# Hyperbolic attention of a four-layer model: constant products added on TensorE, the second batch's scores and turns reordered

## The chip, the cores and the metric

The kernel is one program on one core of a Trainium2 chip. Its time is the device time of one execution in microseconds (us), and of several executions the median. The engines are called PE (matmul), DVE (vector), ACT (scalar functions), POOL (GpSimd) and SP (which issues transfers).

## The reference, cut to what matters

A model of four layers, each with cross attention, self attention and a feed-forward block, on B = 2 sequences of T = 256 tokens and 256 channels. The change touches one block of it, the self attention of layer 1, with H = 16 heads of 16 channels:

```python
importance = jax.nn.sigmoid(x @ Wimp.T + bimp)
spikes = (importance > spike_threshold).astype(x.dtype)
spike_mask = spikes.reshape(B, 1, T, 1)
...
scores_euclid = jnp.einsum('bhtd,bhsd->bhts', q, k) / math.sqrt(D)
...
q_hyp = _expmap0(qn)
k_hyp = _expmap0(kn)
inner = -jnp.einsum('bhti,bhsi->bhts', q_hyp[..., :1], k_hyp[..., :1]) + jnp.einsum('bhtd,bhsd->bhts', q_hyp[..., 1:], k_hyp[..., 1:])
mdot = jnp.maximum(-inner, 1.0 + 1e-06)
dist = jnp.arccosh(mdot)
scores_hyper = -(dist * dist) / curv_k
scores = (1.0 - alpha) * scores_euclid + alpha * scores_hyper
scores = jnp.where(causal[None, None], scores, -jnp.inf)
attn = jax.nn.softmax(scores, axis=-1) * spike_mask
y = jnp.einsum('bhts,bhsd->bhtd', attn, v)
return y @ Wout.T + bout
```

## The kernel before, in words

`hyperbolic_attention` projects q, k, v and the gates, maps q and k to points of the hyperboloid, and turns them so that channels lie on partitions (`turned["qE"]`, `["kE"]` the plain ones, `["qH"]`, `["kH"]` the points). Then `hyperbolic_softmax` makes everything from the inner products to the scaled y. It is one stage: each engine has a program written out by hand, and semaphores order them.

Work goes in 16 pairs of heads, 8 to a batch; two pairs make a quad (8 quads). Of a head's 256 x 256 scores the causal part is kept, W = 384 columns: 128 for the first block of queries, 256 for the second. A pair so has 768 columns, in two PSUM banks. `banks` has three such slots. The list `order` says which piece of work takes the next slot ("hyper" products, "plain" scores, "turn"), and `slot_free` waits until the piece three places ahead has been read.

A pair passes these steps. PE multiplies points (L1916, hyper). DVE makes reach, max(m, 1 + 1e-6) - 1, (L1982) and the radicand of arccosh (L1986). ACT takes the root (L2038), POOL adds it (L2028), ACT takes the logarithm (L2043), POOL squares it (L2031). PE puts a constant causal mask (`steps16_q`, 384 columns a head, bf16, L1923) and the plain products (L1916) into a slot. DVE adds the two kinds of score (L2010, four operations) and finds the maxima (L2015, two). ACT takes exponentials (L2062, four). PE turns the six 128 x 128 blocks (L1931), ACT copies them out (L2047). For each quad PE multiplies by v (values, L1942; column 16 of each 32 holds the softmax's sum), ACT copies y (L2053), PE spreads the sums over the rows with a selecting matrix (L1952), and DVE inverts them (L1991), multiplies by the spikes (L1993) and by y (L1995). The spikes were spread at the stage's start by four matmuls (L1955) and an ACT copy (L2072).

The order: PE multiplies the points of all 16 pairs. Then, for each batch, two scores ahead, and for each pair the scores of the pair two on, the turn, and after each second pair values or spread_sums. DVE does all reaches and radicands, then a batch's scorings with a normal() after each second one. ACT does the roots and logarithms of batch 0, the roots of batch 1, the exponentials and copies of batch 0, the logarithms of batch 1, and its exponentials and copies. Roots, logarithms and exponentials each need their own table, loaded when the function changes.

## Time and profile before

| | |
|---|---|
| three executions | 2756.8, 2743.03, 2754.75 us, median 2754.75 |
| profiled execution | 2750.46 us, its span 2748.6 us |
| mean granted clock of PE | 0.895 of full speed |
| busy shares of the span | PE 85%, DVE 53%, ACT 38%, POOL 14% |
| the stage that the change touches | 1557.70 to 1661.90, 104.20 us, 3.8% of the span |

The profile is of one execution. A granted clock of 1.00 is 2.4 GHz, of 0.50 is 1.2 GHz. "x24" behind a row is its count of instructions; a float32 matmul appears twice in it. In a timeline the bracket at the end is the idle time ahead, and what ended it. A window's row gives its stretch and length, the busy us (xcount) of PE, PEld (PE's weight loads), DVE, ACT and POOL, the granted clock, the DMA share and GB/s.

### The profile page before, as it was taken

The numbers are of one execution on the slowest core, as the hardware profiler recorded it, in microseconds if no ns is written. First come the engines' busy times: TensorE is split into PE (matmuls) and PEld (weight loads), VectorE is DVE, ScalarE is ACT, GpSimd is POOL, SyncE is SP. The second block draws the span as 40 slices with busy tenths as digits, with TensorE's granted clock in tenths as the row PEclk, the third lists the DMA queues.
The fourth block names the chain that finished last, engine by engine and source line by source line (L and its number), as shares of the span: only waits on it lengthen the run. The fifth ranks groups of instructions, "written<-read, shape, count | busy, mean of one in ns | idle before, by whom it ended". The sixth has DMA issues, their size and how long they took to land. (4 is left out here: it accounts for less than half of the span.)

```text
span 2748.6 us, 38678 instructions
## 1 busy us (share of the span) xinstructions
PE 2333.9 (85%) x15024; PEld 1363.0 (50%) x15024; DVE 1455.3 (53%) x2285; ACT 1055.1 (38%) x1896; POOL 380.9 (14%) x659
## 2 busy tenths in 40 slices
PE   3999999868999698999996684886889799697778
PEld 1344444435699463454443443352238557364447
DVE  4777777423221356888883684225877332223333
ACT  2566666512111233777774371123432133021310
POOL 2453000000000400000001250001630000000100
PEclk8899999978899897999998777886989899898889
DMA  7977543020353698556430001001004430200200
GB/s 192 237 183 160 119 90 58 12 96 1 138 229 140 221 281 244 108 93 127 93 59 34 12 1 59 28 1 63 0 19 166 168 123 1 96 1 2 99 1 8
DMA packets 108213, 258.59 MB, mean 94 GB/s; under 512 B 11808, under 2 KB 83072, under 8 KB 94080
## 3 DMA queue, kind: packets, MB, share of 16 engines
q1 hardware_dynamic: 101696, 203.71, 28.2%
q0 software_dynamic: 2736, 39.37, 4.2%
...
## 5 line engine op out<-in xcount | busy, mean ns | idle before, releaser
L666 DVE TENSOR_REDUCE sta_parts<-sta_psA 128x1 f32<-128x1024 f32 x544 | 625.6, 1187 | 188.6 <-PE sta_psA L583 186.8
L724 ACT ACTIVATE sta_probs<-sta_psS 128x512 f32<-128x512 f32 x1056 | 575.8, 597 | 274.9 <-PE sta_psS L594 272.8
L594 PE MATMUL sta_psS<-L_xattn_qS,L_xattn_kst 99*128 99x256 bf16 x2112 | 356.3, 278 | 11.5 <-ACT sta_probs L724 6.6
L583 PE MATMUL sta_psA<-L_xattn_kst,L_xattn_qS 99*128 99x512 bf16 x1088 | 293.3, 387 | 46.9 <-PEq L59 32.1
L594 PEld LDWEIGHTS sta_psS<-L_xattn_qS,L_xattn_kst 99*128 99x128 bf16 x2112 | 161.4, 98 | 259.5 <-ACT sta_probs L724 183.3
L603 PE MATMUL sta_psO<-sta_probs,L_xattna_V 128*32 128x256 f32 x2560 | 189.5, 385 | 0.0
L583 PEld LDWEIGHTS sta_psA<-L_xattn_kst,L_xattn_qS 99*128 99x128 bf16 x1088 | 104.3, 99 | 131.7 <-DVE sta_parts L666 43.7
L202 ACT ACT_TABLE_LOAD x14 | 18.0, 1283 | 327.7 <-PEq L59 327.7
L603 PE MATMUL sta_psO<-sta_probs,L_xattn_V 128*32 128x256 f32 x1536 | 114.8, 390 | 0.0
L1008 ACT ACTIVATE sht_probs<-sht_psS 128x768 f32<-128x768 f32 (+1 forms) x64 | 55.3, 863 | 148.8 <-PE sht_psS L852 99.7
L443 POOL CAST sta_split<-sta_neg 128x2 bf16<-128x2 f32 x64 | 12.1, 188 | 715.9 <-issue 467.5
L603 PEld LDWEIGHTS sta_psO<-sta_probs,L_xattna_V 128*32 128x32 f32 x2560 | 82.4, 109 | 51.4 <-issue 20.9
L2415 POOL TENSOR_TENSOR l2t_u<-l2s_rowsB,l2s_dx 128x512 f32<-128x512 f32 x64 | 80.2, 1266 | 139.7 <-POOLq L59 99.3
L953 DVE TENSOR_REDUCE sht_neg<-sht_psM 128x2 f32<-128x512 f32 (+1 forms) x128 | 69.3, 583 | 41.4 <-PE sht_psM L845 41.4
L2385 PE MATMUL l2t_psY<-l2t_hc,top_consts_weights 128*128 128x512 f32 x128 | 77.0, 699 | 15.0 <-DVE l2t_hc L2431 14.9
L823 POOL MEMSET sht_Z<- 128x512 bf16 x4 | 2.1, 526 | 593.0 <-POOLq L59 593.0
L2424 DVE TENSOR_TENSOR_SCAN l2t_h<-l2t_decay,l2t_u 128x512 f32<-128x512 f32 x64 | 76.4, 1214 | 11.7 <-ACT l2t_decay L2397 9.3
L255 PE MATMUL gem_banks<-3f_L_ffn_experts_weights,l3f_hT 128*128 128x256 f32 x288 | 64.3, 387 | 12.4 <-PEq L59 12.4
L1710 DVE TENSOR_TENSOR l0f_inner_hT<-exp_psG,l0f_inner_gel 128x512 f32<-128x512 f32 x22 | 15.2, 691 | 97.4 <-ACT l0f_inner_gel L1636 97.4
L255 PEld LDWEIGHTS gem_banks<-3f_L_ffn_experts_weights,l3f_hT 128*128 128x128 f32 x288 | 56.0, 195 | 21.1 <-issue 13.2
L603 PEld LDWEIGHTS sta_psO<-sta_probs,L_xattn_V 128*32 128x32 f32 x1536 | 49.5, 110 | 31.8 <-issue 14.0
L1170 PE MATMUL prj_psV<-L_xattn_L_xattn_weights,L_xattnq_cxT 128*128 128x256 f32 x256 | 59.9, 388 | 4.9 <-DVE prj_rows L1210 4.9
...
## 6 DMA issues: line engine op xcount, KB each, us to landing
...
L_xattna_V<-L_xattn_values SPq DMA_DIRECT2D x5, 2048.0 KB, 11.1
...
```

What stands on the lines that cost most here:

```text
L255: last = nc.tensor.matmul(view(n), *term, start=i == 0, stop=i == len(terms) - 1)
L583: last = nc.tensor.matmul(psA[:, u % 2, col:col + rhs.shape[1]], lhsT, rhs, start=True, stop=True)
L594: last = nc.tensor.matmul(psS[:, at % 2, j * T:(j + 1) * T], lhsT, rhs, start=True, stop=True)
L603: last = nc.tensor.matmul(psO[32 * group:32 * group + 32, 0:T], v, probs[:, u % NP, col:col + T], start=first, stop=final)
L666: nc.vector.tensor_reduce(into(parts[:, u // n % 2]), view(psA[:, u % 2, :]), AX.X, ALU.max).then_inc(max_taken, 1)
L724: nc.scalar.activation(probs[:, u % NP, i * 512:(i + 1) * 512], psS[:, at % 2, :], ACT.Exp, scale=scale).then_inc(probs_ready, 1)
L953: last = nc.vector.tensor_reduce(neg[:, g % 2, t, 2 * (u % 2):2 * (u % 2) + 2], psM[:, u % 2, :, at:at + w], AX.X, ALU.max, negate=True)
L1008: nc.scalar.activation(probs[:, u % NP, :, 0:W], psS[:, :, 0:W], ACT.Exp, scale=scale).then_inc(probs_ready, 1)
L1170: last = nc.tensor.matmul(psV[:, v % VRING, j * C:(j + 1) * C], cxT[b][:, k, t * P:(t + 1) * P], w["v"][:, k, 0:C], start=k == 0, stop=k = ...
L2385: nc.tensor.matmul(psY[:, m, :], K["ident"], hc[:, i % 3, :], start=s == 0, stop=s == NS - 1).then_inc(summed, 1)
L2415: nc.gpsimd.tensor_tensor(u[:, i % 3, :], rowsB[:, s % ROWS, :], dx[:, m, :], ALU.mult).then_inc(input_ready, 1)
L2424: nc.vector.tensor_tensor_scan(h[:, i % 3, :], decay[:, i % 2, :], u[:, i % 3, :], 0.0, ALU.mult, ALU.add).then_inc(states_ready, 1)
```

## The change: what it does

1. The spread spikes go. The sums are inverted as columns: two matmuls of 4 columns (`sums`, into the free part of psY), a reciprocal of 8 columns and two products with the spikes (`invert`), an ACT copy that repeats each value 32 times (`widen`), two matmuls that turn the result (`spread`), and one product on DVE (`scale`). psY and psN have one buffer each.
2. `fill` multiplies a constant by a constant, bf16, 384 columns; nothing reads the result. Two follow each pair of points, two stand ahead of each of the second batch's scores, and twelve ahead of each batch's first turn.
3. The mask is added on the diagonal blocks only, 4 x 128 columns a pair.
4. The second batch's scores and scorings stand together beside its logarithms, all its turns after them, and the copies of its turns are on DVE (`copied_by_dve`) rather than ACT.

```diff
-    order = [("hyper", k) for k in range(PAIRS)]
-    for b in range(B):
-        own = range(b * HALF, (b + 1) * HALF)
-        order += [("plain", own[0]), ("plain", own[1])]
-        for k in own:
-            order += [("plain", k + 2)] * (k + 2 in own) + [("turn", k)]
+    order = [("hyper", k) for k in range(PAIRS)] + [("plain", 0), ("plain", 1)]
+    for k in range(HALF):
+        order += [("plain", k + 2)] * (k + 2 < HALF) + [("turn", k)]
+    order += [("plain", k) for k in range(HALF, PAIRS)] + [("turn", k) for k in range(HALF, PAIRS)]
...
-        spikesT = p.sb("spikesT", [P, NTOK])
         yP = p.sb("yP", [P, 2, T])
-        inverse = p.sb("inverse", [P, 2, T])
+        inverse = p.sb("inverse", [P, 2, TB, 4])
+        wide = p.sb("wide", [P, 2, T])
         banks = p.ps("banks", [P, 2 * SLOTS, 512])
-        psY = p.ps("psY", [P, 2, T])
-        psN = p.ps("psN", [P, 2, T])
+        psY = p.ps("psY", [P, 512])
+        psN = p.ps("psN", [P, T])
...
+                def fill(dst, n):
+
+                    for _ in range(n):
+                        nc.tensor.matmul(dst, K["ident16"], K["mask16_q"][:, 0:W], start=True, stop=True)
...
+                def points(k):
+                    slot_free("hyper", k)
+                    dst = pair("hyper", k)
                     for t in range(TB):
                         for j in range(2):
-                            r = slice(64 * half + 32 * j, 64 * half + 32 * j + 32)
-                            last = nc.tensor.matmul(dst[:, j, cols[t]], q[r, c, (b * TB + t) * P:(b * TB + t + 1) * P],
-                                                    k[r, c, b * T:b * T + (t + 1) * P], start=first, stop=first or t == TB - 1)
-                    return last
+                            last = product(dst, turned["qH"], turned["kH"], k, j, t, start=True, stop=True)
+                    last.then_inc(hyper_ready, 1)
+                    fill(psY[:, 0:W], 2)
 
                 def scores(k):
                     slot_free("plain", k)
+                    dst = pair("plain", k)
+                    if k >= HALF:
+                        fill(dst[:, 0, :], 2)
                     for j in range(2):
-                        nc.tensor.matmul(pair("plain", k)[:, j, :], K["ident16"], K["steps16_q"], start=True, stop=False)
-                    products(pair("plain", k), turned["qE"], turned["kE"], k, False).then_inc(plain_ready, 1)
+                        product(dst, turned["qE"], turned["kE"], k, j, 1, start=True, stop=False)
+                    for j in range(2):
+                        nc.tensor.matmul(dst[:, j, 2 * P:W], K["ident16"], K["steps16_q"][:, 2 * P:W], start=False, stop=True)
+                    for j in range(2):
+                        nc.tensor.matmul(dst[:, j, 0:P], K["ident16"], K["steps16_q"][:, 0:P], start=True, stop=False)
+                    for j in range(2):
+                        last = product(dst, turned["qE"], turned["kE"], k, j, 0, start=False, stop=True)
+                    last.then_inc(plain_ready, 1)
 
                 def turn(k):
                     slot_free("turn", k)
+                    if k % HALF == 0:
+                        fill(pair("turn", k)[:, 0, :], 12)
                     pe.wait_ge(exp_ready, k + 1)
...
+                    copied(2 * g + 1)
                     if g:
                         pe.wait_ge(y_copied, g)
+                        pe.wait_ge(inverse_in, g)
...
+                def sums(g):
+
                     pe.wait_ge(y_copied, g + 1)
+                    for t in range(TB):
+                        last = nc.tensor.matmul(psY[:, T + 4 * t:T + 4 * t + 4], yP[:, g % 2, t * P:(t + 1) * P], K["col32"], start=True, stop=True)
+                    last.then_inc(sums_ready, 1)
+
+                def spread(g):
+                    pe.wait_ge(widened, g + 1)
                     if g:
-                        pe.wait_ge(inverted, g)
-                    else:
-                        pe.wait_ge(spikes_copied, 1)
-                    nc.tensor.matmul(psN[:, g % 2, :], K["sel32"], yP[:, g % 2, :], start=True, stop=True).then_inc(spread_ready, 1)
-
-                for t in range(NT):
-                    last = nc.tensor.matmul(psN[:].rearrange("p a n -> p (a n)")[:, t * P:(t + 1) * P], spikes[:, t:t + 1].to_broadcast([P, P]), K["ident"],
-                                            start=True, stop=True)
-                last.then_inc(spikes_spread, 1)
+                        pe.wait_ge(scaled, g)
+                    for t in range(TB):
+                        last = nc.tensor.matmul(psN[:, t * P:(t + 1) * P], wide[:, g % 2, t * P:(t + 1) * P], K["ident"], start=True, stop=True)
+                    last.then_inc(spread_ready, 1)
...
+                    points(k)
+                scores(0)
+                scores(1)
+                for k in range(HALF):
+                    if k + 2 < HALF:
+                        scores(k + 2)
+                    turn(k)
+                    if k % 2 == 0 and k:
+                        values(k // 2 - 1)
+                    if k % 2 == 0 and k > 2:
+                        spread(k // 2 - 2)
+                    if k % 2 and k > 1:
+                        sums((k - 3) // 2)
+                values(QHALF - 1)
+                spread(QHALF - 2)
+                scores(HALF)
+                sums(QHALF - 1)
+                scores(HALF + 1)
+                scores(HALF + 2)
+                spread(QHALF - 1)
+                for k in range(HALF + 3, PAIRS):
+                    scores(k)
+                for k in range(HALF, PAIRS):
+                    g = k // 2
+                    turn(k)
+                    if k % 2 == 0 and k > HALF:
+                        values(g - 1)
+                    if k % 2 == 0 and k > HALF + 2:
+                        spread(g - 2)
+                    if k % 2 and k > HALF + 1:
+                        sums(g - 1)
+                values(QUADS - 1)
+                spread(QUADS - 2)
+                sums(QUADS - 1)
+                spread(QUADS - 1)
...
+                def invert(g):
+                    b = g // (QUADS // B)
+                    dve.wait_ge(sums_ready, g + 1)
+                    V.reciprocal(inverse[:, g % 2], psY[:, T:T + 4 * TB].rearrange("p (t h) -> p t h", t=TB)).then_inc(inverse_in, 1)
+                    dve.wait_ge(inverse_in, g + 1)
+                    for t in range(TB):
+                        last = V.tensor_scalar(inverse[:, g % 2, t], inverse[:, g % 2, t], spikes[:, b * TB + t:b * TB + t + 1], None, ALU.mult)
+                    last.then_inc(inverted, 1)
+
+                def scale(g):
                     b, c = g // (QUADS // B), g % (QUADS // B)
                     dve.wait_ge(spread_ready, g + 1)
-                    V.reciprocal(inverse[:, g % 2, :], psN[:, g % 2, :]).then_inc(inverted, 1)
-                    dve.wait_ge(inverted, g + 1)
-                    V.tensor_tensor(inverse[:, g % 2, :], inverse[:, g % 2, :], spikesT[:, b * T:(b + 1) * T], ALU.mult).then_inc(inverse_ready, 1)
-                    dve.wait_ge(inverse_ready, g + 1)
-                    V.tensor_tensor(attT[:, c, b * T:(b + 1) * T], yP[:, g % 2, :], inverse[:, g % 2, :], ALU.mult).then_inc(scaled, 1)
+                    V.tensor_tensor(attT[:, c, b * T:(b + 1) * T], psN[:], yP[:, g % 2, :], ALU.mult).then_inc(scaled, 1)
...
+                def copy_turned(k):
+                    dve.wait_ge(turn_ready, k + 1)
+                    V.tensor_copy(both(R, k), pair("turn", k)).then_inc(copied_by_dve, 1)
+
+                for k in range(HALF):
+                    scored(k)
+                    if k % 2 == 0 and k >= 4:
+                        invert(k // 2 - 2)
+                    if k % 2 == 0 and k >= 6:
+                        scale(k // 2 - 3)
+                invert(QHALF - 2)
+                scale(QHALF - 3)
+                scale(QHALF - 2)
+                scored(HALF)
+                scored(HALF + 1)
+                invert(QHALF - 1)
+                for k in range(HALF + 2, PAIRS):
+                    scored(k)
+                    if k == HALF + 4:
+                        scale(QHALF - 1)
+                for k in range(HALF, PAIRS):
+                    copy_turned(k)
+                    if k % 2 == 0 and k >= HALF + 4:
+                        invert(k // 2 - 2)
+                    if k % 2 == 0 and k >= HALF + 6:
+                        scale(k // 2 - 3)
+                invert(QUADS - 2)
+                scale(QUADS - 3)
+                scale(QUADS - 2)
+                invert(QUADS - 1)
+                scale(QUADS - 1)
...
+                def widen(g):
+                    act.wait_ge(inverted, g + 1)
+                    nc.scalar.copy(wide[:, g % 2, :].rearrange("p (x n) -> p x n", n=32),
+                                   inverse[:, g % 2].rearrange("p t h -> p (t h)").unsqueeze(2).to_broadcast([P, 4 * TB, 32])).then_inc(widened, 1)
+
+                def weights(k):
+                    act.wait_ge(top_ready, k + 1)
+                    for j in range(2):
+                        for t in range(TB):
+                            one = D[:, 2 * k + j, cols[t]]
+                            last = nc.scalar.activation(one, one, ACT.Exp, bias=top[:, k, t, j:j + 1])
+                    last.then_inc(exp_ready, 1)
+
                 roots(0)
-                logarithms(0)
+                logarithms(range(HALF))
                 roots(1)
-                weights(0)
-                logarithms(1)
-                weights(1)
+                for k in range(HALF):
+                    weights(k)
+                    if k:
+                        copy_turned(k - 1)
+                        if k % 2 and k > 1:
+                            copy_y((k - 3) // 2)
+                        if k % 2 and k >= 5:
+                            widen((k - 5) // 2)
+                copy_turned(HALF - 1)
+                widen(QHALF - 2)
+                logarithms(range(HALF, HALF + 1))
+                copy_y(QHALF - 1)
+                logarithms(range(HALF + 1, HALF + 4))
+                widen(QHALF - 1)
+                logarithms(range(HALF + 4, PAIRS))
+                for k in range(HALF, PAIRS):
+                    g = k // 2
+                    weights(k)
+                    if k % 2 and k > HALF + 1:
+                        copy_y(g - 1)
+                    if k % 2 and k >= HALF + 5:
+                        widen(g - 2)
+                widen(QUADS - 2)
+                copy_y(QUADS - 1)
+                widen(QUADS - 1)
```

PE at the stage's start. Before, the spike matmuls and then the points' products:

```order
L1955 MATMUL hyp_psN<-top_consts_weights,l1a_spikes 128x128 x4
L1916 MATMUL hyp_banks<-l1a_T_kH,l1a_T_qH 128x128 x2
L1916 MATMUL hyp_banks<-l1a_T_kH,l1a_T_qH 128x256 x2
L1916 MATMUL hyp_banks<-l1a_T_kH,l1a_T_qH 128x128 x2
L1916 MATMUL hyp_banks<-l1a_T_kH,l1a_T_qH 128x256 x2
```

Now, the same products (L1928) with two constants (L1923) behind each pair's:

```order
L1928 MATMUL hyp_banks<-l1a_T_kH,l1a_T_qH 128x128 x2
L1928 MATMUL hyp_banks<-l1a_T_kH,l1a_T_qH 128x256 x2
L1923 MATMUL hyp_psY<-top_mask,top_ident 128x384 x2
L1928 MATMUL hyp_banks<-l1a_T_kH,l1a_T_qH 128x128 x2
L1928 MATMUL hyp_banks<-l1a_T_kH,l1a_T_qH 128x256 x2
L1923 MATMUL hyp_psY<-top_mask,top_ident 128x384 x2
```

The spikes' four are gone, and each pair's block is followed by 768 columns of constants.

PE in the second batch. Before, a score (L1923, L1916), a turn (L1931), and after each second pair values (L1942) or spread (L1952):

```order
L1931 MATMUL hyp_banks<-top_consts_weights,hyp_D 128x128 x6
L1942 MATMUL hyp_psY<-hyp_R,l1a_v 32x256 x4
L1942 MATMUL hyp_psY<-hyp_R,l1a_v 32x128 x4
L1923 MATMUL hyp_banks<-top_steps,top_ident 128x384 x2
L1916 MATMUL hyp_banks<-l1a_T_kE,l1a_T_qE 128x128 x2
L1916 MATMUL hyp_banks<-l1a_T_kE,l1a_T_qE 128x256 x2
L1931 MATMUL hyp_banks<-top_consts_weights,hyp_D 128x128 x6
L1952 MATMUL hyp_psN<-hyp_yP,top_consts_weights 128x256
```

Now, the end of its last score, the twelve constants, the first three turns in a row, and the first values and sums (L1982):

```order
L1928 MATMUL hyp_banks<-l1a_T_kE,l1a_T_qE 128x256 x2
L1948 MATMUL hyp_banks<-top_steps,top_ident 128x128 x2
L1950 MATMUL hyp_banks<-top_steps,top_ident 128x128 x2
L1928 MATMUL hyp_banks<-l1a_T_kE,l1a_T_qE 128x128 x2
L1923 MATMUL hyp_banks<-top_mask,top_ident 128x384 x12
L1962 MATMUL hyp_banks<-top_consts_weights,hyp_D 128x128 x18
L1974 MATMUL hyp_psY<-hyp_R,l1a_v 32x256 x4
L1974 MATMUL hyp_psY<-hyp_R,l1a_v 32x128 x4
L1962 MATMUL hyp_banks<-top_consts_weights,hyp_D 128x128 x6
L1982 MATMUL hyp_psY<-top_consts_weights,hyp_yP 128x4 x2
```

All eight scores of the batch now stand ahead of its first turn.

DVE at the end of the second batch. Before, the last scoring's two last additions (L2010), its maxima (L2015) and the normalisations:

```order
L2010 SCALAR_TENSOR_TENSOR hyp_D<-hyp_R,l1a_coef,hyp_banks 128x128
L2010 SCALAR_TENSOR_TENSOR hyp_D<-hyp_R,l1a_coef,hyp_banks 128x256
L2015 TENSOR_REDUCE hyp_top<-hyp_D 128x2 x2
L1991 RECIPROCAL hyp_inverse<-hyp_psN 128x256
L1993 TENSOR_TENSOR hyp_inverse<-hyp_inverse,hyp_spikesT 128x256
L1995 TENSOR_TENSOR l1a_attT<-hyp_yP,hyp_inverse 128x256
```

Now, all eight copies of turns (L2078) behind the last scoring, among inverses (L2045, L2048) and a scale (L2054):

```order
L2068 SCALAR_TENSOR_TENSOR hyp_D<-hyp_R,l1a_coef,hyp_banks 128x256
L2073 TENSOR_REDUCE hyp_top<-hyp_D 128x2 x2
L2078 COPY hyp_R<-hyp_banks 128x768 x5
L2045 RECIPROCAL hyp_inverse<-hyp_psY 128x8
L2048 TENSOR_SCALAR hyp_inverse<-hyp_inverse,l1a_spikes 128x4 x2
L2078 COPY hyp_R<-hyp_banks 128x768 x2
L2045 RECIPROCAL hyp_inverse<-hyp_psY 128x8
L2048 TENSOR_SCALAR hyp_inverse<-hyp_inverse,l1a_spikes 128x4 x2
L2054 TENSOR_TENSOR l1a_attT<-hyp_psN,hyp_yP 128x256
```

The first inverse of the batch stands behind five copies.

## Rows read from the trace of the kernel before

**Rows 1.** Windows of the stage: busy us (xcount) by engine, clock, DMA share, GB/s

```profile
1557.70:1594.30 36.60, 30.93 (x166) 17.17 (x167) 34.05 (x48) 25.49 (x33) 30.18 (x19) 0.57 0.07 22
1594.30:1620.74 26.44, 23.04 (x168) 14.31 (x168) 19.77 (x40) 17.42 (x40) 9.69 (x6) 0.75 0.00 1
1620.74:1661.90 41.16, 28.24 (x202) 17.00 (x202) 34.45 (x66) 28.31 (x54) 11.80 (x8) 0.79 0.00 1
```

**Rows 2.** Timeline of PE at the stage's start: start, us, engine, line

```profile
1558.01 1.13 PE L1955 MATMUL hyp_psN<-top_consts_weights,l1a_spikes 128*128 128x128 f32 x8 [1.05 <-PEq L59]
1559.07 1.58 PE L1916 MATMUL hyp_banks<-l1a_T_kH,l1a_T_qH 32*128 32x128 f32 x24
```

**Rows 3.** Timeline of DVE, the first hyper operation and the first scoring

```profile
1560.04 1.82 DVE L1982 TENSOR_SCALAR hyp_D<-hyp_banks 128x768 f32<-128x768 f32 x2 [2.35 <-PE hyp_banks L1916]
...
1588.41 1.38 DVE L2010 SCALAR_TENSOR_TENSOR hyp_D<-hyp_R,l1a_coef,hyp_banks 128x128 f32<-128x128 f32 x4
```

**Rows 4.** Timeline of PE: scores, turns, a spread and values at either clock

```profile
1585.95 0.82 PE L1923 MATMUL hyp_banks<-top_steps,top_ident 128*128 128x384 bf16 x2 [0.19 <-DVE hyp_R L1986]
...
1588.29 0.82 PE L1923 MATMUL hyp_banks<-top_steps,top_ident 128*128 128x384 bf16 x2
...
1594.32 1.51 PE L1931 MATMUL hyp_banks<-top_consts_weights,hyp_D 128*128 128x128 f32 x6 [1.30 <-ACT hyp_D L2062]
...
1605.63 0.88 PE L1931 MATMUL hyp_banks<-top_consts_weights,hyp_D 128*128 128x128 f32 x6
1606.34 0.60 PE L1952 MATMUL hyp_psN<-hyp_yP,top_consts_weights 128*128 128x256 f32 x2
...
1608.86 0.86 PE L1942 MATMUL hyp_psY<-hyp_R,l1a_v 128*32 128x256 f32 x16
...
1621.42 0.49 PE L1923 MATMUL hyp_banks<-top_steps,top_ident 128*128 128x384 bf16 x2
...
1622.70 0.50 PE L1923 MATMUL hyp_banks<-top_steps,top_ident 128*128 128x384 bf16 x2
```

**Rows 5.** Windows, columns as in rows 1, for the granted clock

```profile
1563.30:1585.90 22.60, 20.70 (x102) 11.34 (x98) 22.46 (x27) 15.99 (x19) 21.78 (x14) 0.50 0.00 1
1585.95:1592.90 6.95, 6.95 (x30) 3.17 (x30) 6.88 (x15) 6.92 (x10) 6.95 (x5) 0.50 0.00 0
1620.90:1625.30 4.40, 4.39 (x32) 2.27 (x32) 4.30 (x5) 4.39 (x5) 2.25 (x2) 1.00 0.01 4
1768.70:1771.40 2.70, 2.62 (x20) 1.29 (x20) 1.02 (x2) 1.28 (x1) 0.52 (x1) 0.98 0.62 177
1771.50:1774.00 2.50, 0.24 (x3) 0.25 (x4) 0.96 (x2) 0.00 (x0) 0.87 (x4) 0.50 1.01 381
```

**Rows 6.** Timeline of ACT at the second batch's start and the stage's end

```profile
1620.74 1.28 ACT L2043 ACT_TABLE_LOAD   x1
1622.04 6.71 ACT L2043 ACTIVATE hyp_D<-hyp_D,top_consts_weights 128x768 f32<-128x768 f32 x8
...
1630.06 2.88 ACT L2062 ACTIVATE hyp_D<-hyp_D,hyp_top 128x128 f32<-128x128 f32 x8
...
1657.84 0.37 ACT L2053 COPY hyp_yP<-hyp_psY 128x256 f32<-128x256 f32 x1 [0.98 <-PE hyp_psY L1942]
```

**Rows 7.** Timeline of DVE around the second batch's start

```profile
1620.80 0.42 DVE L1993 TENSOR_TENSOR hyp_inverse<-hyp_inverse,hyp_spikesT 128x256 f32<-128x256 f32 x1
...
1623.41 1.38 DVE L1993 TENSOR_TENSOR hyp_inverse<-hyp_inverse,hyp_spikesT 128x256 f32<-128x256 f32 x1
...
1626.32 1.38 DVE L2010 SCALAR_TENSOR_TENSOR hyp_D<-hyp_R,l1a_coef,hyp_banks 128x128 f32<-128x128 f32 x4
1627.74 1.01 DVE L2015 TENSOR_REDUCE hyp_top<-hyp_D 128x2 f32<-128x256 f32 x2
```

**Rows 8.** Groups by form, busy us and mean ns of one: small operations elsewhere

```profile
L969 DVE RECIPROCAL sht_inverse<-sht_psT 128x16 f32<-128x16 f32 x10 | 2.6, 258 | 22.9 <-PE sht_psT L914 22.9
...
L914 PE MATMUL sht_psT<-top_consts_weights,l0a_attT 128*128 128x4 f32 x32 | 4.9, 280 | 0.5 <-ACT l0a_attT L994 0.5
```

106 lines of the change are left out of this document (38 added, 68 removed).

## The prediction

> **What bounds the kernel now.** I read the windows first. The change touches one stage of a kernel with some dozens of stages, the hyperbolic softmax, which lasts from 1557.70 to 1661.90 us: 104.2 us. Cut at its first turn and at the table load of the second batch's logarithms it falls into A 36.60, B 26.44 and C 41.16 us [rows 1]. Whatever the change does has to come out of these. No engine fills all three: DVE is busy 34.05 of 36.60 us in A, 19.77 of 26.44 in B and 34.45 of 41.16 in C [rows 1]. So DVE bounds A, and B and C are hand-overs between PE, DVE and ACT.
>
> The timeline of A shows DVE going without a gap from the first hyper operation at 1560.04 to the first scoring at 1588.41 [rows 3]; that is 32 operations (two a pair) in 28.37 us, 0.89 us each, so 1.77 us a pair; from 1563.30 to 1585.90 it is busy 22.46 of 22.60 us [rows 5]. PE works at 1.2 GHz there (granted 0.50) and just keeps up. Its pieces have two prices: a score piece (two constants of 384 columns and a pair's products) takes 2.34 us at 1.2 GHz (1585.95 to 1588.29) and 1.28 at 2.4 GHz (1621.42 to 1622.70); six turns take 1.51 or 0.88 [rows 4]. So the clock decides whether the longer PE programme hides.
>
> **The change, part A.** The four spike matmuls go: the first product stood at 1559.07 behind their start at 1558.01 [rows 2], so all starts 1.06 us sooner, DVE at 1558.98. Then each pair gets two constants behind its products. These are the same constants and the same number of products as a score piece, so the price is 2.34 or 1.28 us against DVE's 1.77. At 2.4 GHz it is hidden (the cover is DVE; the first scoring then comes at 1558.98 + 28.37 = 1587.35, 1.1 us sooner); at 1.2 GHz it is not, and PE becomes the bound.
>
> Will the clock hold? Three rows speak. Pieces of this very make, back to back, kept 2.4 GHz while they lasted: 1620.90 to 1625.30, granted 1.00. The same pieces at 1.2 GHz, PE busy 6.95 of 6.95 us, did not raise it: granted 0.50 from 1585.95 to 1592.90. And in a later stage two such pieces in 2.70 us ran at 0.98 and the granted clock was 0.50 right behind them [rows 5]. Paced by DVE the new pieces come at most two in 3.54 us, thinner than that last case. So I expect the clock to fall while the points run, as it did before, only some pairs later, and then not to come back as long as nothing but such pieces runs. The Trainium skill (TensorE: Matmul & The Clock Gate, Part 1) says that the default state is throttled and activity releases it, and advises to keep TensorE busy; read simply, filling PE with constants would hold 2.4 GHz. The row of 6.95 busy us at 0.50 is the case in this trace that does not follow from being busy alone. What holding it would give is the first rival.
>
> I take six pairs before the fall: three ahead at 1.28 (to 1561.8), three at DVE's pace (to 1567.1), then ten at 2.34, to 1590.5. A new score piece has the same products and two thirds of the constants' columns: 2.34 less a third of the 0.82 of its two constants [rows 4], 2.1 us (bounds 1.28 and 2.34). The first scoring starts at 1592.5 instead of 1588.41, and three pieces end at 1596.8. Ahead of the first turn come twelve more constants: from 0.49 / 2 = 0.25 each at 2.4 GHz to 0.82 / 2 = 0.41 each at 1.2 [rows 4], so 2.9 to 4.9 us; I take 4.1, since the rows' durations hold an end that overlaps with the next. The first turn starts at 1600.9 instead of 1594.3. ACT's exponentials are ready sooner than that (first scoring 1592.5 + 2.4 + 1.4), so PE is what is late. **A: +6.5.**
>
> **Part B.** The constants lie dense ahead of the turns, and I give them the clock back: turns, values and spreads at 2.4 GHz where the first three turns were at 1.2. The normalisation changes from reciprocal and two products over 256 columns (DVE) to a tiny sum on PE (two matmuls of about 0.28), a reciprocal of 8 columns (bounded by 0.26 for 16), two small products, a widening copy on ACT (256 columns, like copy_y's 0.37) and two spread matmuls [rows 4, 6, 8]. DVE's part shrinks, but the chain now goes through PE and ACT twice, psY is one buffer (values(g) waits for the reciprocal of g-1), and spread(g) and invert(g) stand in queues ahead of scores and scorings. A clock gain of at most 3 turns x 0.63 + 3 pieces x 1.06 = 5.1 stands against those hand-overs; I take them as equal (bounds -4 and +3).
>
> The two small products read and write SBUF alone, and POOL, with the second batch's sums, is still busy for 9.69 us of B [rows 1]. A 256-column product between SBUF operands took 0.42 us at 1620.80 and 1.38 at 1623.41, when POOL had begun its squares (2.25 us of POOL end the window that closes at 1625.30) [rows 5, 7]. I take +1.0 for it. The Trainium skill (SBUF — State Buffer, Who interferes with whom) has this as a rule: a DVE instruction with two SBUF inputs or in a two-port mode waits for GpSimd's whole instruction. The trace agrees (0.42 against 1.38). **B: +1.0** (bounds -4 and +4).
>
> **Part C.** The second batch's scorings move beside its logarithms, the turns' copies to DVE, all after the last scoring. Step by step at 2.4 GHz, from the table load:
> First scoring: load 1.28, first logarithm 0.84 (6.71 / 8), a square, which lies between 0 and 3.4 (5.58 us from load to first scoring before [rows 6, 7], less 2.1) and which I take as 1.5, hand-overs 0.2: 3.8.
> Eight scorings of 1.38 + 1.01 less 0.05 of overlap [rows 7]: 18.8, and 1.5 for an inverse, a scale and a wait for logarithms behind widen: 20.3.
> Tail. ACT has exponentials 8 to 11 behind it, then copy_y(4), and everything behind that waits: copy_y(4) needs values(4), values(4) needs two copies that DVE starts only now. Two copies 1.9 (one bounded by DVE's 0.91 on as many PSUM columns [rows 3]), values 0.86, copy_y 0.37, four exponentials 1.44, turn 0.88, copy 0.95, hand-overs 0.5: first inverse after 6.9. Each further quad goes round values 0.86, copy_y 0.37, widen 0.4, spread 0.5, turn 0.88, two copies 1.9 less overlap 0.1, inverse 0.3 [rows 3, 4, 6, 8]: 5.1, twice. Last: values, copy_y, sum, inverse, widen, spread, scale, 4.0. Tail 21.1.
> Sum 45.2 against 41.16: +4.0 even at 2.4 GHz, since DVE's work is not less and the tail is a chain.
> Now the clock. While scoring, PE has two constants (0.75) and a 2.1 us piece per pair at 1.2 GHz, 2.9 against DVE's 2.35: eight are 23.2, +3.4 with the waits beside. By the argument of A these are thin pieces of the same make at DVE's pace, so I take 1.2 GHz. In the tail each loop has 0.63 for a turn more at 1.2 GHz, as much for values and some 0.4 for a spread (an estimate, by the same ratio), 1.7 a loop; twelve constants stand ahead of it, so I take one loop of the three, +1.6. **C: +9.0.**
>
> **Sum.** 6.5 + 1.0 + 9.0 = +16.5. The profiled execution took 2750.46 us (span 2748.6), 4.3 below the median of the runs shown (2743.03 to 2756.8, mean 2751.5): 2767.0. DMA and other stages aren't touched. What moves behind the stage is only where the clock's changes fall, a few us of either sign.
>
> **The rivals.**
> Clock held: 2.4 GHz throughout, as the rule above and the row 1620.90 to 1625.30 suggest. A -1.1, B 0, C +4.0: 2753. Against it the row behind 1771.4. It decides as soon as nine of the ten late pairs run at 1.28.
> Constants never bring the clock back, also not ahead of the turns: A +7.3 (twelve at 0.41), B +6 (eight turns x 0.63 and two spreads), C +11 (a second loop): 2775. For it speaks that 6.95 busy us did not raise it; against it that those had the thin products, and twelve constants have not.
> Overlap pays (the other side): the tail isn't a chain but DVE's own work, 8 x 0.9 + 4 x 0.9 = 11, in place of 21, and the clock holds: C -6, A -1.1, and B at its lower bound -4: -11.1, 2739. It needs ACT to get past copy_y(4) within 1 us of the last scoring; the order rows say that it can't.
> No effect: clock held in A alone, lost in C: A -1.1, B +1, C +9: 2759.
>
> **How the numbers follow.** Chances: forecast 0.50 (its own range +10 to +23), held 0.22, never back 0.12, mixed 0.10, overlap pays 0.06. 0.5% is 13.8 us, about what a measurement of this kernel tells from no change. Of the forecast two thirds lie above it, and all of "never back": slower 0.33 + 0.12 + 0.01 = 0.46. Held, mixed and the forecast's lower third: same 0.47. Faster 0.07. The range leaves out the far ends of the outer rivals: 2746 to 2781.
>
> **What would show it.** In the profile after: DVE's first scoring near 1592, not 1587; granted clock falling to 0.50 between 1566 and 1570 and PE without gaps until about 1600; first turn near 1601; in C an ACT gap of some 8 us ahead of a copy_y while DVE copies; stage length about 120 us. Wrong if the granted clock stays 1.00 through the points, if the second batch's tail is under 15 us, or if a stage outside moves.

## The result, and the profile after

The changed kernel takes 2767.36 us (median of 8, 2762.27 to 2778.03), the kernel before 2750.44 (median of 8). The ratio is 1.0073, with a 95% interval of 1.0054 to 1.0091: slower by some 20 us by the ratio, 17 by the medians. A second set of the same program gave 1.0096 (1.0073 to 1.0119). The forecast was 2767.0.

The profiled execution took 2762.76 us (span 2760.8, clock 0.898). Its stage runs from 1554.12 to 1683.23: 129.1 us, against 104.2. Cut where [rows 1] are cut, and with the pairs at the lower clock as a fourth row (columns as there), the windows of the changed kernel are:

```profile
1554.12:1595.77 41.65, 39.95 (x209) 18.81 (x210) 35.33 (x50) 26.60 (x35) 35.47 (x22) 0.63 0.07 20
1595.77:1624.41 28.64, 21.74 (x185) 16.02 (x187) 14.36 (x42) 16.38 (x39) 4.36 (x3) 0.85 0.00 1
1624.41:1683.23 58.82, 50.68 (x292) 31.52 (x284) 31.42 (x77) 24.05 (x52) 11.48 (x8) 0.62 0.00 1
1564.90:1592.30 27.40, 27.34 (x128) 12.59 (x126) 22.77 (x32) 21.05 (x26) 26.57 (x17) 0.50 0.00 1
```

A is 41.65 us against 36.60, B 28.64 against 26.44, C 58.82 against 41.16. DVE's (VectorE's) busy time fell in B (14.36 against 19.77) and C (31.42 against 34.45), yet both grew: DVE waits more. In all, +24.9 us against a forecast of +16.5, of which C makes 17.7. That the total came out as forecast is partly luck. The stage starts 3.6 us sooner in this execution, and what lies behind it is 9 us shorter, though the edit doesn't touch either. The windows from the stage's end to the same table load in a later layer, and from there to the end, of the changed kernel and then of the kernel before:

```profile
1683.23:2058.18 374.95, 287.60 (x1056) 124.26 (x1056) 200.43 (x300) 101.92 (x150) 87.69 (x97) 0.87 0.08 28
2058.18:2760.80 702.62, 583.17 (x3096) 412.46 (x3096) 259.50 (x661) 151.65 (x256) 15.52 (x67) 0.88 0.18 67
```

```profile
1661.90:2046.95 385.05, 300.55 (x1056) 129.83 (x1056) 200.31 (x300) 101.91 (x149) 87.75 (x97) 0.82 0.07 27
2046.95:2748.60 701.65, 582.94 (x3096) 411.80 (x3096) 259.36 (x661) 151.64 (x256) 15.52 (x67) 0.89 0.18 67
```

TensorE's counts are the same, and in the first window the granted clock is 0.87 instead of 0.82, for 10.1 us less. So the forecast had the stage 8.4 us too short, and what lies outside it made up for that. It does not do so reliably: over the fourteen traces of this document the span less the stage lies anywhere from 2632 to 2651 us, though no edit touches what is in it. The kernel before lies between 2737.9 and 2756.8 us by itself. Below I therefore compare stages, and give the ratio beside.

Part A, TensorE's timeline of the changed kernel, where the clock falls:

```profile
1562.88 0.50 PE L1923 MATMUL hyp_psY<-top_mask,top_ident 128*128 128x384 bf16 x2
1563.75 0.92 PE L1928 MATMUL hyp_banks<-l1a_T_kH,l1a_T_qH 32*128 32x128 f32 x8 [0.37 <-DVE hyp_R L2040]
1564.61 0.81 PE L1923 MATMUL hyp_psY<-top_mask,top_ident 128*128 128x384 bf16 x2
1565.48 1.65 PE L1928 MATMUL hyp_banks<-l1a_T_kH,l1a_T_qH 32*128 32x128 f32 x8
1567.07 0.82 PE L1923 MATMUL hyp_psY<-top_mask,top_ident 128*128 128x384 bf16 x2
1567.82 1.65 PE L1928 MATMUL hyp_banks<-l1a_T_kH,l1a_T_qH 32*128 32x128 f32 x8
```

Two constants take 0.50 us up to the sixth pair, 0.81 behind the seventh (1564.61) and 0.82 from there on; from there TensorE has no gap, and each pair takes 2.34 us (1565.48 to 1567.82). Twelve constants at 1592.32 take 3.61 us and the clock is back: the turns behind them take 0.82 to 0.88 us.

Part B, DVE's inverses in the changed kernel, with what they waited for:

```profile
1604.31 0.21 DVE L2045 RECIPROCAL hyp_inverse<-hyp_psY 128x8 f32<-128x8 f32 x1 [1.52 <-PE hyp_psY L1982]
1604.56 0.36 DVE L2048 TENSOR_SCALAR hyp_inverse<-hyp_inverse,l1a_spikes 128x4 f32<-128x4 f32 x2
...
1614.06 0.21 DVE L2045 RECIPROCAL hyp_inverse<-hyp_psY 128x8 f32<-128x8 f32 x1 [4.46 <-PE hyp_psY L1982]
...
1623.35 0.21 DVE L2045 RECIPROCAL hyp_inverse<-hyp_psY 128x8 f32<-128x8 f32 x1 [6.02 <-PE hyp_psY L1982]
```

They come 9.8 and 9.3 us apart, and DVE is idle 4.46 and 6.02 us ahead of them. On ACT and on TensorE in the same place:

```profile
1607.29 1.49 ACT L2151 ACTIVATE hyp_D<-hyp_D,hyp_top 128x128 f32<-128x128 f32 x4 [2.29 <-DVE hyp_top L2073]
...
1609.37 0.36 ACT L2139 COPY hyp_yP<-hyp_psY 128x256 f32<-128x256 f32 x1
1609.63 0.41 ACT L2143 COPY hyp_wide<-hyp_inverse 128x256 f32<-128x256 f32 x1
```

```profile
1607.07 0.86 PE L1974 MATMUL hyp_psY<-hyp_R,l1a_v 128*32 128x256 f32 x16
1610.09 0.71 PE L1990 MATMUL hyp_psN<-top_consts_weights,hyp_wide 128*128 128x128 f32 x4 [2.16 <-ACT hyp_wide L2143]
...
1612.11 1.27 PE L1962 MATMUL hyp_banks<-top_consts_weights,hyp_D 128*128 128x128 f32 x6
1613.17 0.86 PE L1982 MATMUL hyp_psY<-top_consts_weights,hyp_yP 128*128 128x4 f32 x4
...
1620.16 1.22 PE L1990 MATMUL hyp_psN<-top_consts_weights,hyp_wide 128*128 128x128 f32 x4 [3.74 <-ACT hyp_wide L2143]
```

The wait goes round: the inverse waits for sums (L1982), which stand behind spread (L1990), the next score and a turn; spread waits for widen (L2143); widen stands behind the exponentials of pair 5 and a copy of y; and those exponentials wait for a scoring that stands behind the inverse before.

Part C, DVE in the changed kernel, from the last two scorings on:

```profile
1650.79 1.39 DVE L2068 SCALAR_TENSOR_TENSOR hyp_D<-hyp_R,l1a_coef,hyp_banks 128x128 f32<-128x128 f32 x4 [0.74 <-PE hyp_banks L1928]
...
1653.96 1.39 DVE L2068 SCALAR_TENSOR_TENSOR hyp_D<-hyp_R,l1a_coef,hyp_banks 128x128 f32<-128x128 f32 x4 [0.74 <-PE hyp_banks L1928]
...
1658.11 2.69 DVE L2078 COPY hyp_R<-hyp_banks 128x768 f32<-128x768 f32 x3 [1.71 <-PE hyp_banks L1962]
...
1664.57 0.20 DVE L2045 RECIPROCAL hyp_inverse<-hyp_psY 128x8 f32<-128x8 f32 x1
...
1671.54 0.20 DVE L2045 RECIPROCAL hyp_inverse<-hyp_psY 128x8 f32<-128x8 f32 x1
...
1676.65 0.20 DVE L2045 RECIPROCAL hyp_inverse<-hyp_psY 128x8 f32<-128x8 f32 x1
...
1682.69 0.43 DVE L2054 TENSOR_TENSOR l1a_attT<-hyp_psN,hyp_yP 128x256 f32<-128x256 f32 x1 [1.75 <-PE hyp_psN L1990]
```

Each scoring waits 0.74 us for TensorE and they come 3.17 us apart. Behind the last one 26.7 us go by, where the kernel before had 8.9.

### The profile page after: what moved, and what is told of

The parts are those of the page before. It is cut to its first block and busy times, and to the rows that moved or that the text cites. A ratio compares the mean times of both kernels' runs of the same rounds, so it can differ in the third digit from the quotient of the medians.

```text
span 2760.8 us, 38981 instructions
## 1 busy us (share of the span) xinstructions
PE 2347.6 (85%) x15168; PEld 1373.2 (50%) x15168; DVE 1448.8 (52%) x2301; ACT 1051.0 (38%) x1895; POOL 380.5 (14%) x659
## 5 line engine op out<-in xcount | busy, mean ns | idle before, releaser
L603 PEld LDWEIGHTS sta_psO<-sta_probs,L_xattna_V 128*32 128x32 f32 x2560 | 82.8, 109 | 52.0 <-issue 21.9
L2488 PE MATMUL l2t_psY<-l2t_hc,top_consts_weights 128*128 128x512 f32 x128 | 73.6, 664 | 16.7 <-DVE l2t_hc L2534 16.5
L255 PE MATMUL gem_banks<-3f_L_ffn_experts_weights,l3f_hT 128*128 128x256 f32 x288 | 64.3, 387 | 12.5 <-PEq L59 12.5
```

The source lines that it names most:

```text
L255: last = nc.tensor.matmul(view(n), *term, start=i == 0, stop=i == len(terms) - 1)
L603: last = nc.tensor.matmul(psO[32 * group:32 * group + 32, 0:T], v, probs[:, u % NP, col:col + T], start=first, stop=final)
L2488: nc.tensor.matmul(psY[:, m, :], K["ident"], hc[:, i % 3, :], start=s == 0, stop=s == NS - 1).then_inc(summed, 1)
```

## The experiments

"Stage" is from TensorE's first instruction of the stage to DVE's last; A ends at the first turn, B at the table load of the second batch's logarithms. Each stage is one traced execution, each ratio is to the kernel before over 6 to 12 executions of the variant, with its interval.

| kernel | A | B | C | stage | ratio |
|---|---|---|---|---|---|
| before | 36.3 | 26.4 | 41.0 | 103.8 | 1 |
| changed | 41.3 | 28.6 | 58.7 | 128.7 | 1.0073 (1.0054 to 1.0091) |
| a_again | 40.2 | 29.1 | 59.6 | 128.8 | 1.0096 (1.0073 to 1.0119) |
| a_nopoints | 36.2 | 28.7 | 58.7 | 123.5 | 1.0061 (1.0038 to 1.0084) |
| a_noscores | 41.1 | 31.0 | 53.4 | 125.5 | 1.0054 (1.0035 to 1.0072) |
| a_nofill | 35.2 | 33.8 | 54.4 | 123.4 | 1.0041 (1.0024 to 1.0058) |
| a_three | 35.4 | 33.5 | 58.7 | 127.5 | 1.0094 (1.0077 to 1.0111) |
| a_exps | 42.3 | 27.8 | 54.3 | 124.4 | 1.0070 (1.0052 to 1.0088) |
| b_points | 36.4 | 26.4 | 41.0 | 103.8 | 1.0001 (0.9987 to 1.0015) |
| b_diag | 36.3 | 27.6 | 42.4 | 106.4 | 1.0013 (0.9999 to 1.0027) |
| n_order | 35.2 | 37.5 | 50.1 | 122.8 | 1.0074 (1.0055 to 1.0094) |
| n_late | 35.2 | 26.8 | 38.9 | 101.0 | 1.0001 (0.9987 to 1.0014) |
| n_late_fill | 42.3 | 22.2 | 45.1 | 109.6 | 1.0017 (0.9997 to 1.0036) |
| b_warm | 36.4 | 21.4 | 41.4 | 99.2 | 0.9993 (0.9974 to 1.0011) |

**The constants, taken out one by one.** a_nopoints:

```diff
-                    fill(psY[:, 0:W], 2)
```

> The changed kernel without the two constants behind each pair's points; all else as changed. Theory (at 1.2 GHz the constants make PE the bound of part A): DVE's 32 operations run without a gap again, the first scoring starts 0.96 + 28.4 us after PE's first product, 5.2 us sooner than in the changed kernel, and the stage is 5 us shorter than its 129.1 us. Rival (the constants cost nothing there, PE would be late anyway because of the clock, or the normal order of scores): the first scoring stays at 34.6 us after the first product. Second rival (the constants feed the clock, so that what follows gets dearer without them): the first scoring is sooner, but part B loses more than 5 us.

A is 5.2 us shorter (the first scoring 29.4 us after the first product, not 34.6), B and C are unchanged: the theory, to the tenth of a microsecond in the stage. The ratios, 1.0073 and 1.0061, can't tell it from nothing.

a_noscores:

```diff
-                    if k >= HALF:
-                        fill(dst[:, 0, :], 2)
```

> The changed kernel without the two constants ahead of each score of the second batch. Theory (each scoring waits for PE, 3.17 us a piece at 1.2 GHz, of which the constants are 0.75): the pieces come each 2.43 us, DVE's own 2.35 nearly bounds them, the eight scorings take 26.9 - 8 x 0.75 = 20.9 us and the stage is 6 us shorter. Rival (the constants keep the clock from being worse, or the scorings wait for the squares): no gain, the scorings keep their distance of 3.17.

The eight scorings take 22.6 us instead of 26.9, C 5.3 less. B is 2.4 us longer, though it ends before the edit's first instruction; its granted clock is 0.77, against 0.85. The stage gains 3.2, half of what was expected.

a_nofill takes out these two and the twelve:

```diff
-                    if k % HALF == 0:
-                        fill(pair("turn", k)[:, 0, :], 12)
```

> The changed kernel with none of its constants: no fill behind points, ahead of scores, or ahead of the turns. Theory (the thin constants only cost, the twelve pay for themselves through the clock): -5 in part A, -6 in the second batch's scorings, the first turns 3 us sooner each but at 1.2 GHz (1.5 us instead of 0.9, values 1.5 instead of 0.86), which gives back some 8 us in parts B and C: stage about 115 to 118 us. Rival (the clock doesn't need the twelve): stage 129.1 - 5 - 6 - 3 - 3.4 = 112 us or less with turns at 0.88. Second rival (order and hand-overs, not the constants, are the cost): stage above 120 us.

123.4 us: neither the 115 to 118 of the theory nor 112, but the second rival. A and C fall by 6.1 and 4.3, and B rises by 5.1, with a granted clock of 0.65 instead of 0.85: without the twelve the first turns start at 1.2 GHz. All constants together cost 5.3 us of the 24.9; the other 19.6 are elsewhere.

**Does the clock fall among the points by the program?** b_points puts the constants into the kernel before:

```diff
                     products(pair("hyper", k), turned["qH"], turned["kH"], k, True).then_inc(hyper_ready, 1)
+                    for _ in range(2):
+                        nc.tensor.matmul(psY[:].rearrange("p a n -> p (a n)")[:, 0:W], K["ident16"], K["mask16_q"][:, 0:W], start=True, stop=True)
```

> The kernel before with only two constants of 384 columns (bf16) behind each pair's points. Theory: PE needs 2.34 us a pair at 1.2 GHz against DVE's 1.77, with the clock falling after about seven pairs, so the first scoring comes 5 us later after PE's first product than in the kernel before (30.4 us) and the stage takes 109 us instead of 104.2. Rival (the clock holds at 2.4 GHz, where the pair costs 1.28): the stage keeps 104 us or is 2 us shorter, since the first turns run at 2.4 GHz.

The rival. The window of its points, and that of a_three below:

```profile
1560.48:1587.09 26.61, 21.55 (x161) 10.18 (x161) 25.31 (x30) 16.83 (x20) 21.44 (x14) 1.00 0.10 30
```

```profile
1561.08:1588.50 27.42, 24.73 (x181) 12.07 (x182) 25.96 (x30) 16.90 (x20) 22.10 (x14) 1.00 0.10 29
```

Granted 1.00 throughout. In b_points these are the same pieces as in the changed kernel, three close together and then one each 1.73 us; there the clock fell behind the seventh. But nothing is won: DVE bounds A, TensorE then waits 4.35 us for the exponentials, and the first turns run at 1.2 GHz all the same.

a_three:

```diff
-                    fill(psY[:, 0:W], 2)
+                    fill(psY[:, 0:W], 3)
```

> The changed kernel with three constants instead of two behind each pair's points. Two executions with two constants ended differently: the clock fell after the seventh pair in the changed kernel, and held to the last pair in the kernel before with the same pieces. Theory (more constants keep the clock safely at 2.4 GHz, and then PE's 1.5 us a pair hides behind DVE's 1.73): granted 1.00 to the last pair, first scoring 29.4 us after the first product instead of 34.6, stage 5 us shorter. Rival (it falls all the same): PE needs 2.72 us a pair at 1.2 GHz, the first scoring comes at 38 us or later and the stage is 3 to 4 us longer.

The theory on A: 35.4 us. But B is 33.5 instead of 28.6 (granted 0.66 there, not 0.85), so that only 1.2 us of the stage is left of it, and the ratio is no better. The twelve constants are in this run too, so they don't secure the clock of B by themselves. B's instructions are the same in six of these runs, and its length goes with its granted clock: 27.8 us at 0.93 (a_exps), 28.6 and 28.7 at 0.85 (changed, a_nopoints), 29.1 at 0.78 (a_again), 31.0 at 0.77 (a_noscores), 33.5 at 0.66 (a_three).

a_again is the changed kernel, unaltered.

> The changed kernel once more, for a second execution with a trace. Theory (the clock among the points hangs on where the pieces fall, not on the program alone): the stage may come out either at about 129 us with the clock falling among the points, or at 124 to 128 with the clock held there; parts B and C keep 27 to 34 and 58 to 59 us. Rival (the program alone decides): the same fall after the seventh pair, 41.3, 28.6 and 58.7 us again within 0.5.

The clock falls again, one pair later, and the parts agree within 1.2 us: more than the 0.5 of the rival, and no execution with the clock held, which the theory allowed. It fell behind the sixth, seventh or eighth pair in all five traces of a stage that starts with points and has two constants a pair (changed, a_again, a_noscores, a_exps, n_late_fill), and in neither of the two that start with the spikes' matmuls (b_points, b_warm). What in the start decides is open.

**The tail.** a_exps:

```diff
                 for k in range(HALF, PAIRS):
-                    g = k // 2
                     weights(k)
+                for k in range(HALF, PAIRS):
+                    g = k // 2
                     if k % 2 and k > HALF + 1:
                         copy_y(g - 1)
```

> The changed kernel with ACT's second batch in another order: the exponentials of all eight pairs first, then its copies of y and widenings. Theory (in the tail everything waits for exponentials that stand behind copy_y(4) and copy_y(5) on ACT, 2.88 us for two pairs each time): the tail of 26.7 us falls to 16 to 19, the stage from 128.7 to about 119. Rival (the tail is the chain of values, copy, sum, inverse, widen and spread alone): tail 25 us or more, stage unchanged within 2 us. Second rival (DVE, which starts its eight copies only behind the last scoring, sets the tail): the tail keeps 8 x 0.9 + the last chain, also below 19, and no wait of DVE is left between its copies.

My theory fell: the tail is 24.7 us, 2 less. The stage is 4.3 shorter, more than the rival's 2, but 2.4 us of it lie ahead of the tail: from the table load to the end of the last scoring 29.6 us instead of 32.0, at a granted clock of 0.62 instead of 0.50. DVE's timeline in a_exps shows why:

```profile
1662.22 2.69 DVE L2078 COPY hyp_R<-hyp_banks 128x768 f32<-128x768 f32 x3 [1.98 <-PE hyp_banks L1962]
1665.80 2.01 DVE L2078 COPY hyp_R<-hyp_banks 128x768 f32<-128x768 f32 x2 [0.89 <-PE hyp_banks L1962]
1667.73 0.20 DVE L2045 RECIPROCAL hyp_inverse<-hyp_psY 128x8 f32<-128x8 f32 x1
...
1671.12 2.01 DVE L2078 COPY hyp_R<-hyp_banks 128x768 f32<-128x768 f32 x2 [2.79 <-PE hyp_banks L1962]
1673.05 0.20 DVE L2045 RECIPROCAL hyp_inverse<-hyp_psY 128x8 f32<-128x8 f32 x1
```

With the exponentials long done, these two inverses still come 5.3 us apart (7.0 in the changed kernel), and a wait of 2.79 us stands between the copies. The next turn is late for another reason: on TensorE it stands behind values, which waits 1.25 us for the inverse (psY is one buffer), and behind spread, which waits 0.79 us for ACT's widening.

**What of the other 19.6 us?** Step by step from the kernel before. b_diag has the mask's change alone, with `product` as in the change:

```diff
-                        nc.tensor.matmul(pair("plain", k)[:, j, :], K["ident16"], K["steps16_q"], start=True, stop=False)
-                    products(pair("plain", k), turned["qE"], turned["kE"], k, False).then_inc(plain_ready, 1)
+                        product(dst, turned["qE"], turned["kE"], k, j, 1, start=True, stop=False)
+                    for j in range(2):
+                        nc.tensor.matmul(dst[:, j, 2 * P:W], K["ident16"], K["steps16_q"][:, 2 * P:W], start=False, stop=True)
+                    for j in range(2):
+                        nc.tensor.matmul(dst[:, j, 0:P], K["ident16"], K["steps16_q"][:, 0:P], start=True, stop=False)
+                    for j in range(2):
+                        last = product(dst, turned["qE"], turned["kE"], k, j, 0, start=False, stop=True)
+                    last.then_inc(plain_ready, 1)
```

> The kernel before with only the mask's change: constants on the diagonal blocks alone (4 x 128 columns a pair instead of 2 x 384), the products in the new order. Theory (a piece takes 1.7 to 2.4 us instead of 2.34 at 1.2 GHz and 1.0 instead of 1.28 at 2.4, but DVE's scorings bound it): part A 0 to -1 us, B and C unchanged within 1 us each, stage 102 to 104 us, ratio 1.000. Rival (fewer dense columns let the clock fall more): B and C up by some us, since turns and values run at 1.2 GHz.

106.4, above the 102 to 104 of the theory: B and C are 1.2 and 1.4 us longer, the side of the rival, with a granted clock of 0.70 and 0.76 against 0.75 and 0.79. The ratio can't tell it from nothing.

n_order is a_nofill with the second batch in the manner of the first on all engines; so it is b_diag plus the new normalisation, and minus the spikes' four matmuls at the start (A 1.1 us less). Its TensorE part (DVE and ACT likewise, all copies of turns by ACT):

```diff
+                for b in range(B):
+                    first, end = b * HALF, (b + 1) * HALF
+                    scores(first)
+                    scores(first + 1)
+                    for k in range(first, end):
+                        if k + 2 < end:
+                            scores(k + 2)
+                        turn(k)
+                        if k % 2 == 0 and k > first:
+                            values(k // 2 - 1)
+                        if k % 2 == 0 and k > first + 2:
+                            spread(k // 2 - 2)
+                        if k % 2 and k > first + 1:
+                            sums((k - 3) // 2)
```

> The changed kernel with no constants and with the second batch in the manner of the first: scores two ahead, turns between, copies of turns by ACT. So it is the kernel before plus the new normalisation and the mask on the diagonal alone. Theory (the reordering makes the tail of 27 us, against 8.9 before, and saves no time in the scorings): C falls from the 54.4 us of the changed kernel without constants to 41 to 45, stage about 110 to 114 us, where the rest over 104 is the new normalisation's chain in B. Rival (the new normalisation's chain makes the tail, in whatever order): C stays above 50.

The theory fell, and this is the run that settled most: with the reordering undone the stage is 122.8, within 0.6 us of a_nofill. C is 50.1, the side of the rival, and B is 37.5. The tail behind the last scoring is 12.5 us, against 27.3 in a_nofill, but the eight scorings take 33.8 against 22.6: the order decides where the waiting stands, and here not how much there is. The ratios of the two, 1.0074 (1.0055 to 1.0094) and 1.0041 (1.0024 to 1.0058), lie further apart than the stages do; the rest is outside the stage. The new normalisation costs 16.4 us over b_diag (one trace each), with the second batch in the first's manner.

n_late moves where its steps stand, and nothing else:

```diff
-                        if k % 2 == 0 and k > first + 2:
-                            spread(k // 2 - 2)
                         if k % 2 and k > first + 1:
                             sums((k - 3) // 2)
+                        if k % 2 and k > first + 3:
+                            spread((k - 5) // 2)
...
-                        if k % 2 == 0 and k >= first + 4:
-                            invert(k // 2 - 2)
-                        if k % 2 == 0 and k >= first + 6:
-                            scale(k // 2 - 3)
+                        if k % 2 and k >= first + 5:
+                            invert((k - 5) // 2)
+                        if k % 2 and k >= first + 7:
+                            scale((k - 7) // 2)
```

> The order of n_order (no constants, second batch in the manner of the first, new normalisation) with three places moved one pair later: on TensorE the spread behind the sums of an odd pair instead of ahead of the next score, on DVE the inverse behind the scoring of the odd pair and the scale behind that of the pair two on. Theory (in n_order each quad goes round a loop of 10.1 us: exponentials, copy of y, widen, spread, score, turn, sums, inverse, and only then the next scoring; the new normalisation costs 16.5 us by where its steps stand, not by their work): the loop opens, the inverses come each 6.5 to 7.5 us, B falls from 37.5 to 28 to 31, C from 50.1 to 43 to 46, stage 107 to 113 us. Rival (the chain through one psY, PE and ACT is the cost wherever it stands): B at 35 or more, stage within 3 us of 122.8.

The theory's direction, and more than its 107 to 113 us: 101.0 us, 21.9 less, and the ratios 1.0074 and 1.0001 lie apart. Windows of B and C, of n_order and of n_late:

```profile
1595.68:1633.15 37.47, 29.89 (x200) 21.19 (x200) 16.31 (x48) 18.73 (x44) 9.66 (x6) 0.64 0.00 1
1633.15:1683.28 50.13, 38.17 (x244) 26.27 (x244) 22.92 (x65) 29.64 (x58) 11.44 (x8) 0.60 0.00 1
```

```profile
1590.69:1617.50 26.81, 24.76 (x200) 17.14 (x200) 16.36 (x48) 18.62 (x44) 9.67 (x6) 0.80 0.01 2
1617.50:1656.41 38.91, 31.64 (x244) 21.03 (x244) 22.97 (x65) 29.55 (x58) 11.44 (x8) 0.73 0.00 1
```

Counts and DVE's busy time are the same (16.31 and 16.36 us in B). What went is waiting, and with it the lower clock: 0.64 to 0.80 and 0.60 to 0.73. How much of the 21.9 us the higher clock made by itself these runs don't separate; the edit is what set both going. The inverses on DVE, first n_order's, then n_late's:

```profile
1609.01 0.21 DVE L2023 RECIPROCAL hyp_inverse<-hyp_psY 128x8 f32<-128x8 f32 x1 [3.01 <-PE hyp_psY L1976]
...
1619.10 0.21 DVE L2023 RECIPROCAL hyp_inverse<-hyp_psY 128x8 f32<-128x8 f32 x1 [4.82 <-PE hyp_psY L1976]
...
1628.40 0.21 DVE L2023 RECIPROCAL hyp_inverse<-hyp_psY 128x8 f32<-128x8 f32 x1 [6.02 <-PE hyp_psY L1976]
```

```profile
1605.25 0.20 DVE L2023 RECIPROCAL hyp_inverse<-hyp_psY 128x8 f32<-128x8 f32 x1
...
1610.75 0.20 DVE L2023 RECIPROCAL hyp_inverse<-hyp_psY 128x8 f32<-128x8 f32 x1
...
1614.01 0.21 DVE L2023 RECIPROCAL hyp_inverse<-hyp_psY 128x8 f32<-128x8 f32 x1 [2.34 <-PE hyp_psY L1976]
```

Distances of 10.1 and 9.3 us became 5.5 and 3.3, and two of the three stand there without a wait.

n_late_fill adds the constants behind points and the twelves to it:

```diff
                     last.then_inc(hyper_ready, 1)
+                    fill(psY[:, 0:W], 2)
...
                     slot_free("turn", k)
+                    if k % HALF == 0:
+                        fill(pair("turn", k)[:, 0, :], 12)
```

> n_late with the changed kernel's constants behind points (two a pair) and ahead of the first turn of each batch (twelve). Theory (the twelve give the clock back at the first turns, worth some 5 us in B if the clock then stays, and cost 3 us where they stand in the second batch, where they hold back a turn that is ready): stage within 2 us of n_late. Rival (constants pay once the hand-overs are out): 4 us or more shorter than n_late. Other rival (the clock falls among the points as in the changed kernel): 5 us longer.

The other rival: 8.6 us longer, since the clock fell among the points again (A 7.1 more). B is 4.6 us shorter (22.2 against 26.8, granted 0.99 against 0.80), as the twelve were to do. C is 6.2 longer, but not because they held back a turn: the turn behind them still waited 1.63 us for its exponentials. The granted clock of C is 0.62 against 0.73; why it fell there is open. The ratio, 1.0017 (0.9997 to 1.0036), can't tell the run from the kernel before.

b_warm is b_points with this ahead of the first turn:

```diff
+                        if k == 0:
+                            for _ in range(18):
+                                nc.tensor.matmul(psY[:].rearrange("p a n -> p (a n)")[:, 0:W], K["ident16"], K["mask16_q"][:, 0:W], start=True, stop=True)
                         turn(k)
```

> The kernel before with two constants behind each pair's points and eighteen ahead of the first turn, where TensorE waited 4.35 us in the run with the points' constants alone. Theory (they fill a wait and hold 2.4 GHz into part B): A within 0.5 us of 36.3, B 2 to 4 us shorter than 26.4 since its first three turns and scores run at 2.4 GHz, C unchanged, stage 100 to 102 us. Rival (DVE or ACT bound B, so that a faster TensorE only waits): stage 103 to 104. Other rival (the clock falls among the points this time): A 5 us or more longer.

The theory, and somewhat more: B is 5.0 us shorter at a granted clock of 1.00, the stage 99.2. TensorE of b_warm:

```profile
1591.78 3.10 PE L1972 MATMUL hyp_psY<-top_mask,top_ident 128*128 128x384 bf16 x18
1596.19 0.85 PE L1931 MATMUL hyp_banks<-top_consts_weights,hyp_D 128*128 128x128 f32 x6 [1.32 <-ACT hyp_D L2067]
1596.88 0.49 PE L1923 MATMUL hyp_banks<-top_steps,top_ident 128*128 128x384 bf16 x2
```

The eighteen fill the wait and the first turn takes 0.85 us, not 1.51. In the whole kernel it isn't to be told from before (0.9993, 0.9974 to 1.0011): seven of its twelve executions lie from 2734.7 to 2739.6 us, four from 2749.8 to 2756.4. It and n_late have the shortest stages; the two together weren't tried, nor was a second buffer for psY.

## Why the prediction was right, and where it was not

Direction, size and range of the total held; the sum behind it holds in part, and the stage outgrew it, 24.9 us against 16.5. That the median, 2767.36, met the 2767.0 to the half microsecond is luck. Of the prediction's own signs, the first scoring (34.6 us behind the first product, 34.5 forecast), the fall of the clock and the tail over 15 us came true. The stage of about 120 us did not (129.1), and "a stage outside moves", named there as a sign of being wrong, did happen: 9 us behind the stage, at the same instructions.

- **A, +6.5: measured +5.0, by the path that was forecast.** The clock fell after seven pairs (six were taken), then 2.34 us a pair as read from [rows 4]; the twelve took 3.6 us (4.1 taken) and gave the clock back. The step "I expect the clock to fall" held for this program, but not for the pieces as such: b_points and a_three held 1.00. So the thinness of the pieces, argued from the row at 1771.4 in [rows 5], didn't decide it. A score piece took 1.69 us in A, not 2.1, and 2.43 in C, where constants stand between.
- **B, +1.0: measured +2.2, within the bounds, as the difference of two large terms.** "I take them as equal" set a clock gain of at most 5.1 us against the hand-overs. a_nofill against the changed kernel gives 5.1 for the first. The rest of the change costs 7.4 without it (a_nofill's 33.8 against the 26.4 before), of which the mask has 1.2 (b_diag). I named the queues and didn't follow the loop once round: with the second batch in the first's manner, moving three steps takes 10.7 us off B (n_order's 37.5, n_late's 26.8). The +1.0 for products beside POOL didn't occur: two of them take 0.36 us at 1604.56. The rule of the Trainium skill (SBUF — State Buffer, Who interferes with whom) had nothing to act on there, since POOL had ended its sums at 1600.1 in this trace.
- **C, +9.0: measured +17.7.** The first scoring stands 5.1 us behind the load (3.8 taken), the scorings take 26.9 (23.7), the tail 26.7 (22.7). In the sum, a scoring's piece was costed at 2.1 + 0.75 = 2.9; it took 3.17. The tail's parts, up to the inverses at 1664.57, 1671.54 and 1676.65 and to the end, are 8.2, 7.0, 5.1 and 6.5 us, against 6.9, 5.1, 5.1 and 4.0 in the sum and 1.6 for the clock. The step left out, between the first two inverses, the exponentials of pairs 14 and 15, 2.88 us on ACT; a_exps shows that without them this round takes 5.3. And the lower clock was put into one loop of the tail: the granted clock of the four parts is 0.97, 0.76, 0.73 and 0.50, so it bears on three. The term for the scorings also adds up wrongly by itself: 23.2 is 4.4 above 18.8, not 3.4, so that the waits were in part dropped.
- **"DVE's work is not less and the tail is a chain".** The chain is real. That the reordering made the stage longer is not shown: n_order, without it, has a tail of 12.5 us and is as long all the same. The reordering alone moved the stage by 0.6 us with inverse and spread where they stand. How it would do with n_late's places wasn't tried.
- **The rivals.** "Clock held" came true in A for a_three and then gave its gain back in B. "Never back" didn't. The Trainium skill's advice to keep TensorE busy (TensorE: Matmul & The Clock Gate, Why this matters for your kernels) fits b_warm, whose constants stand in a wait, and not the changed kernel, where 27.34 of 27.40 us busy went at a granted 0.50.

Together: of the 24.9 us, the mask 2.6 (one trace each, unclear), the normalisation as placed 16.4, the reordering 0.6, the constants 5.3. Each is a difference of single traces, the clock's part within it.
